# Residual sums formed in PSUM instead of by VectorE additions, and attention biases added by a product with ones

## The reference

```
x = x + 0.5 * moe(layernorm(x))
x = x + attention(layernorm(x))
x = x + 0.5 * moe(layernorm(x))

moe:  affinity = softmax(x @ gate_w)            # 8 experts
      gating, index = top_k(affinity^T, 128)    # each expert picks 128 tokens of a batch
      out = (silu(x_sel @ Wg) * (x_sel @ Wu)) @ Wd
      result = zeros.at[index].add(out * gating)
attention (16 heads of 8):
      aperture, expression = sigmoid(x @ Wa + ba), sigmoid(x @ We + be)
      inner, outer, v = x @ Wi, x @ Wo, x @ Wv
      attn = softmax(inner outer^T / sqrt(8)) * aperture * expression, normalized again
      result = rotate(attn @ v) @ Wout
```

## Time and profile before

| | us |
|---|---|
| median of 3 runs | 478.99 (478.91 to 479.18) |
| the profiled execution | 479.99 |
| its span | 478.3 |
| TensorE busy | 402.9 (84%) |
| VectorE busy | 387.3 (81%) |
| ScalarE busy | 232.1 (49%) |
| GpSimd busy | 54.1 (11%) |

### The profile page before, as it was taken

The page is one execution under the profiler, slowest core; times in us unless marked ns, Lnnn a source line. Parts: engine busy times, 40 slices in busy tenths (PEclk is TensorE's granted clock), DMA queues, the critical chain, the costliest instruction groups (busy, mean ns, idle before and its releaser), DMA issues.

```text
span 478.3 us, 7748 instructions
## 1 busy us (share of the span) xinstructions
PE 402.9 (84%) x2220; PEld 217.0 (45%) x2220; DVE 387.3 (81%) x877; ACT 232.1 (49%) x439; POOL 54.1 (11%) x103
## 2 busy tenths in 40 slices
PE   2705999999788989999999999999979039999995
PEld 1602556776453543333333333334429014567764
DVE  6698977889789888998899899887545889768883
ACT  2400543341432157777777777778762104443322
POOL 4520002212000010000000000000014400011210
PEclk9999999999897669999999999999995559999999
DMA  6100011223077801111111111100200000112103
GB/s 179 46 0 0 1 34 34 66 66 89 16 276 236 325 29 46 47 46 56 49 54 55 52 45 45 45 1 4 66 1 0 0 1 1 34 33 66 45 23 88
DMA packets 25768, 27.49 MB, mean 57 GB/s; under 512 B 3920, under 2 KB 17488, under 8 KB 25680
## 3 DMA queue, kind: packets, MB, share of 16 engines
q1 hardware_dynamic: 25744, 27.20, 18.6%
HBM read 17.08 MB, written 9.98 MB: 57 GB/s over the span
## 4 chain that ended last, share of the span: by engine, by line
PE 76%; DVE 15%; ACT 4%; issue 2%; DMA 1%; DVEq 0%; ACTq 0%
PE ps L1192 14%; PE ps L1202 13%; PE ps L1177 6%; PE ps L1036 6%; PE ps L1074 6%; PE ps L1057 3%; PE ps L1059 3%; PE ps L1058 3%; DVE heads_out L726 3%; DVE neg_max L839 3%; DVE values L723 3%; PE ps L1089 3%; PE ps L1090 3%; PE ps L992 3%; ACT probs L616 2%
## 5 line engine op out<-in xcount | busy, mean ns | idle before, releaser
L839 DVE TENSOR_REDUCE neg_max<-ps 128x1 f32<-128x512 f32 x256 | 160.9, 679 | 14.5 <-PE ps L1177 14.4
L616 ACT ACTIVATE probs<-ps 128x512 f32<-128x512 f32 x256 | 136.8, 601 | 44.1 <-PE ps L1192 42.9
L1177 PE MATMUL ps<-stacks 63*128 63x512 f32 x256 | 106.1, 494 | 3.3 <-DVE neg_max L839 2.4
L1192 PE MATMUL ps<-stacks 64*128 64x512 f32 x256 | 95.1, 463 | 4.7 <-ACT probs L616 4.6
L1192 PEld LDWEIGHTS ps<-stacks 64*128 64x128 f32 x256 | 41.2, 189 | 76.3 <-ACT probs L616 65.6
L1202 PE MATMUL ps<-probs,v_ext 128*32 128x512 f32 x512 | 69.0, 612 | 0.0
L1177 PEld LDWEIGHTS ps<-stacks 63*128 63x128 f32 x256 | 43.6, 195 | 20.0 <-DVE neg_max L839 15.7
L532 ACT CAST stacks<-ps 128x512 fp32r<-128x512 f32 x32 | 17.2, 589 | 67.2 <-PE ps L1036 67.2
L769 DVE TENSOR_TENSOR probs<-slot_row,slot 128x512 f16<-128x512 f16 x64 | 39.2, 681 | 0.1
L458 POOL TENSOR_TENSOR w_lo<-w_gu,w_hi 128x512 fp32r<-128x512 f32 x16 | 20.3, 1275 | 146.2 <-ACT w_hi L517 146.2
L794 DVE TENSOR_TENSOR vae_and_gates<-heads_out,ps 128x512 f32<-128x512 f32 x32 | 21.7, 685 | 16.1 <-ACT heads_out L540 8.3
(11 more groups left out here) (152 smaller groups left out, 556.3 us busy)
## 6 DMA issues: line engine op xcount, KB each, us to landing
stacks<-parts_dram SPq DMA_DIRECT2D x64, 128.0 KB, 2.4
parts_dram<-part_hi SPq DMA_DIRECT2D x8, 512.0 KB, 3.5
parts_dram<-part_lo SPq DMA_DIRECT2D x8, 512.0 KB, 5.2
w_gu<-in_L_ffn_Wg_dram SPq DMA_DIRECT2D x16, 128.0 KB, 2.1
w_gu<-in_L_ffn_Wu_dram SPq DMA_DIRECT2D x16, 128.0 KB, 2.1
wd_sb<-in_L_ffn_Wd_dram SPq DMA_DIRECT2D x16, 128.0 KB, 2.2
x<-in_L_attn_x_dram SPq DMA_DIRECT2D x4, 256.0 KB, 3.7
stacks<-k_rows_dram SPq DMA_DIRECT2D x2, 512.0 KB, 6.7
```

The costliest lines, as they stand in the source:

```text
L616: nc.scalar.activation(probs[:, u // HG, u % HG, :], ps[:, RING + ring_bank(step, u), :], ACT.Exp, scale=SCORE_SCALE).then_inc(probs_ready, 1)
L839: nc.vector.tensor_reduce(neg_max[:, g, col, qt:qt + 1], ps[:, ring_bank(step, u), :], AX.X, ALU.max, negate=True).then_inc(max_taken, 1)
L1177: nc.tensor.matmul(ps[:, ring_bank(step, u), :], q_stack[rows, g, pp, chunk(qt)], k_stack[rows, g, pp, :], start=True, stop=True).then_inc ...
L1192: nc.tensor.matmul(ps[:, RING + ring_bank(step, u), :], k_stack[rows, g, pp, chunk(c)], q_stack[rows, g, pp, :], start=True, stop=True).th ...
```

## The change

Scatter bank b begins as the transposes of x of batch b (16 transposes in place of four products of zeros), and the factor 0.5 moves to copy_down. So the bank holds x plus half of the expert sums, and the transposes back give the new x in banks 4 to 7 (SUM_BANK + b). There is no add_moe. After the first expert stage VectorE takes statistics and normalizes from these banks, and ScalarE copies them to x (copy_x). TensorE projects in other banks, since the sums lie in 4 to 7, and in another order; VectorE's and ScalarE's lists are reordered. The biases are added by a product of a row of ones with the bias row, 32 columns, behind each of the vae products, and ScalarE copies the result (copy_vae). At the end of attention, batch 3's output bank starts with the product of the identity with x, its statistics and its norm are read from there, and VectorE's copy to x, which gives the fourth x_attended, stands behind norm_apply(2, 3). After the last stage VectorE copies three batches and ScalarE the fourth. TensorE's wait for x_attended ahead of logits(1, 0) stays as it was.

```diff
 copy_down:
-    nc.scalar.copy(down_out[:], ps[:, 6, :]).then_inc(down_copied[l], 1)
+    nc.scalar.mul(down_out[:], ps[:, 6, :], 0.5).then_inc(down_copied[l], 1)
 TensorE, experts, ahead of the loop:
+    if l == 1:
+        pe.wait_ge(x_attended, B)
     for b in range(B):
-        nc.tensor.matmul(ps[:, b, :], zeros[:, 0:P], zeros[:], start=True, stop=True)
+        for c in range(C):
+            nc.tensor.matmul(ps[:, b, chunk(c)], x[:, C * b + c, :], ident[:], is_transpose=True,
+                             start=c == 0, stop=True, skip_group_check=True)
 ScalarE, preparation of attention:
+    def copy_x(l, b):
+        act.wait_ge(moe_turned[l], b + 1)
+        if l == 0:
+            act.wait_ge(xn_ready[1], C * (b + 1))
+        nc.scalar.copy(x[:, b * C:(b + 1) * C, :]..., ps[:, SUM_BANK + b, :]).then_inc(x_copied[l], 1)
     root(1, 0)
+    copy_x(0, 0)
     copy_xnT(1, 0)
     root(1, 1)
+    root(1, 2)
     copy_qk_hi(0)
-    root(1, 2)
+    copy_x(0, 1)
     copy_xnT(1, 1)
+    root(1, 3)
+    copy_x(0, 2)
+    copy_qk_hi(1)
     copy_xnT(1, 2)
-    root(1, 3)
-    copy_qk_hi(1)
+    copy_x(0, 3)
     copy_xnT(1, 3)
+    copy_vae(0)
     copy_qk_hi(2)
+    copy_vae(1)
+    copy_vae(2)
     copy_qk_hi(3)
     copy_max_rows(0, 0)
+    copy_vae(3)
 VectorE, preparation of attention:
+    stats_of_sum(0)
+    norm_apply(1, 0, steps, SUM_BANK)
+    stats_of_sum(1)
+    stats_of_sum(2)
+    norm_apply(1, 1, steps, SUM_BANK + 1)
+    split_qk_lo(0)
+    stats_of_sum(3)
+    norm_apply(1, 2, steps, SUM_BANK + 2)
+    norm_apply(1, 3, steps, SUM_BANK + 3)
     split_qk_lo(1)
-    add_bias(1)
     split_qk_lo(2)
-    add_bias(2)
     take_maxima(0, range(MAX_UNITS))
     split_qk_lo(3)
-    take_maxima(1, range(MAX_UNITS // 2))
-    add_bias(3)
-    take_maxima(1, range(MAX_UNITS // 2, MAX_UNITS))
+    take_maxima(1, range(MAX_UNITS))
 TensorE, preparation of attention:
+    QK_BANKS = ((0, 4), (1, 5), (4, 5), (4, 5))
+    VAE_BANKS = ((2, 6), (3, 7), (3, 6), (6, 7))
     project_vae(b):
-        pe.wait_ge(xnT_ready[1], b + 1)
+        pe.wait_ge(xnT_ready[1], (3, 4, 4, 4)[b])
+        if b < 2:
+            sum_bank_free(2 + b)        # xn_ready of the batch, and x_copied
+        if b > 1:
+            pe.wait_ge(vae_ready, 2 * b)
+            last = nc.tensor.matmul(ps[:, VAE_BANKS[b][w], first + D:first + D + 2 * H], ones_row[:],
+                                    bias_row[0:1, D:], start=False, stop=True, skip_group_check=True)
     turn_xn(1, 0)
     project_qk(0)
     turn_xn(1, 1)
+    project_qk(1)
     turn_xn(1, 2)
+    turn_xn(1, 3)
     project_vae(0)
-    project_qk(1)
+    project_qk(2)
     project_vae(1)
-    turn_xn(1, 3)
-    project_qk(2)
     project_vae(2)
 End of attention:
+    in project_out(3), ahead of its wait for combinedT:
+        nc.tensor.matmul(ps[:, OUT_BANK[b], :], ident[:], x[:, b * C:(b + 1) * C, :]..., start=True, stop=True)
+    in add_attention(3), instead of the add:
+        norm_stats(2, b, norm_steps, OUT_BANK[b])
     norm_apply(2, 2, norm_steps)
-    norm_apply(2, 3, norm_steps)
+    norm_apply(2, 3, norm_steps, OUT_BANK[3])
+    nc.vector.tensor_copy(x[:, 3 * C:, :]..., ps[:, OUT_BANK[3], :]).then_inc(x_attended, 1)
```

More of the change, by code:

```diff
@@ L386, in _ @@
             for b in range(B):
-                sp.wait_ge(x_added[1], b + 1)
+                if b < B - 1:
+                    sp.wait_ge(out_rows_ready, b + 1)
+                else:
+                    sp.wait_ge(x_copied[1], 1)
                 sp.dma_start(out[b].rearrange("(c p) d -> p c d", p=P), x[:, b * C:(b + 1) * C, :]).then_inc(out_stored, 16)
@@ L566, in experts @@
                     act.wait_ge(scattered[l], b + 1)
-                    nc.scalar.mul(moeT[:, b, :], ps[:, b, :], 0.5).then_inc(moeT_ready[l], 1)
+                    nc.scalar.copy(moeT[:, b, :], ps[:, b, :]).then_inc(moeT_ready[l], 1)
             act.wait_ge(eps_made, 1)
@@ L638, in _, with norm_stats @@
             experts(1)
+            copy_x(1, B - 1)
         @block.vector
         def _(dve):
-            def norm_stats(n, b, steps):
+            def norm_stats(n, b, steps, bank=None):
                 tiles = range(b * C, (b + 1) * C)
                 for t in tiles:
-                    steps.did(nc.vector.bn_stats(out=stats[:, t, :], in_=x[:, t, :]))
+                    rows = x[:, t, :] if bank is None else ps[:, bank, D * (t % C):D * (t % C) + D]
+                    steps.did(nc.vector.bn_stats(out=stats[:, t, :], in_=rows))
                 steps.settle()
@@ L649, in norm_stats, with norm_apply @@
                     nc.vector.bn_aggr(out=mean_var[:, t, :], in_=stats[:, t, :]).then_inc(var_ready[n], 1)
-            def norm_apply(n, b, steps):
+            def norm_apply(n, b, steps, bank=None):
                 t0 = slice(b * C, (b + 1) * C)
@@ L656, in norm_apply @@
                 for t in range(b * C, (b + 1) * C):
-                    nc.vector.tensor_scalar(xn[:, t, :], x[:, t, :], mean_var[:, t, 0:1], rstd[:, t:t + 1],
+                    rows = x[:, t, :] if bank is None else ps[:, bank, D * (t % C):D * (t % C) + D]
+                    nc.vector.tensor_scalar(xn[:, t, :], rows, mean_var[:, t, 0:1], rstd[:, t:t + 1],
                                             ALU.subtract, ALU.mult).then_inc(xn_ready[n], 1)
@@ L969, in _ @@
             norm_apply(2, 2, norm_steps)
-            norm_apply(2, 3, norm_steps)
+            norm_apply(2, 3, norm_steps, OUT_BANK[3])
+            nc.vector.tensor_copy(x[:, 3 * C:, :].rearrange("p c d -> p (c d)"), ps[:, OUT_BANK[3], :]).then_inc(x_attended, 1)
             route(1)
             experts(1)
-            for b in range(B):
-                add_moe(1, b)
+            for b in range(B - 1):
+                copy_out_rows(b)
         @block.tensor
@@ L1155, in project_vae @@
                     for c in range(2):
-                        f = slice(c * (D + 2 * H), (c + 1) * (D + 2 * H))
-                        last = nc.tensor.matmul(ps[:, 6 + w, f], xnT[:, b, chunk(2 * w + c)], wvae_sb[:], start=True, stop=True)
+                        first = c * (D + 2 * H)
+                        nc.tensor.matmul(ps[:, VAE_BANKS[b][w], first:first + D + 2 * H], xnT[:, b, chunk(2 * w + c)], wvae_sb[:],
+                                         start=True, stop=True, skip_group_check=True)
+                        last = nc.tensor.matmul(ps[:, VAE_BANKS[b][w], first + D:first + D + 2 * H], ones_row[:], bias_row[0:1, D:],
+                                                start=False, stop=True, skip_group_check=True)
                     last.then_inc(vae_projected, 1)
@@ L1276, in project_out @@
             def project_out(b):
+                if b == B - 1:
+                    nc.tensor.matmul(ps[:, OUT_BANK[b], :], ident[:], x[:, b * C:(b + 1) * C, :].rearrange("p c d -> p (c d)"),
+                                     start=True, stop=True, skip_group_check=True)
                 pe.wait_ge(combinedT_ready, b + 1)
@@ L1280, in project_out @@
                 for c in range(C):
-                    last = nc.tensor.matmul(ps[:, OUT_BANK[b], chunk(c)], combinedT[:, b, chunk(c)], w_rot[:], start=True, stop=True)
+                    last = nc.tensor.matmul(ps[:, OUT_BANK[b], chunk(c)], combinedT[:, b, chunk(c)], w_rot[:], start=b < B - 1, stop=True,
+                                            skip_group_check=b == B - 1)
                 last.then_inc(attention_out, 1)
```

68 lines of the change are left out of this document (32 added, 36 removed).

## The result

| | before | changed |
|---|---|---|
| median, us | 478.96 (478.91 to 479.18) | 500.75 (499.31 to 503.69) |
| profiled execution, its span | 479.99, 478.3 | 500.7, 499.0 |
| TensorE, VectorE busy | 402.9, 387.3 | 421.3, 380.2 |

The changed kernel takes 1.0468 times as long, interval [1.0439, 1.0497]. Forecast were 491.3 and a range that ends at 495.5: the direction was right, the size was not. Six points of the two timelines say where the 20.7 us of span arise. Scatter banks are in the first and the last piece; the second and the third, 15.3 us together, are the preparation of attention, the fifth its end.

The account below looks back on a forecast made before the run. TensorE was taken to bound the kernel, through its chain of waits. Terms 1.8 + 3.75 + 1.5 + 0.8 + 4.6 - 0.1 = 12.35 us on the median of 478.99 gave 491.3, range 484.5 to 495.5.

Parts of the forecast that it names:

- what bounds it: Whole kernel: TensorE ends most steps of the chain of waits; in the preparation of attention VectorE waits.
- scatter banks: Both expert stages: sixteen transposes in place of four products of zeros, nothing hides them, +0.90 us a stage, +1.8 for two.
- the logits waiting for the copy: Ahead of logits(1, 0): TensorE waits for VectorE's copy of x, which gives the fourth x_attended, at 366.3 us.
- the loops' period: Expert loops: the period stays unchanged at 6.8 us (423.61 to 430.38).
- almost nothing at the end of the kernel: After the last stage: three VectorE copies and one ScalarE copy replace four adds, -0.1 us (0 to -0.5).
- Rival 3: Preparation of attention: VectorE is the bound, its lighter load decides and hides TensorE's lateness, 477.9 us; chance 0.05.
- xnT(2): Preparation of attention: ready at 137.7 us, where it was there near 134.3 before.
- The order: Preparation of attention: reordered queues put norm_apply(2) behind the split of qk(0) and make xnT(2) late; 1.05 us beside the products.
- the price of the products with ones: project_vae: eight added instructions at 0.11 us each, half hidden, 0.9 a vae (0.3 to 1.7).
- the clock: Preparation of attention: TensorE perhaps at half clock when vae(0) and qk(2) come, +0.8 us (0 to +3).
- The bound itself: Upper price for a product with ones: 0.21 us an instruction at full clock, from logits with float32 stationaries and 8 columns.
- End of attention: From batch 3's output bank to the logits: the copy of x comes late and the whole delay goes through, +4.6 us (3.7 to 5.8).

## Why the prediction missed

- **Right:** what bounds it (TensorE, not VectorE, in the preparation); scatter banks; the logits waiting for the copy; the loops' period (444.34 to 451.11); almost nothing at the end of the kernel. Rival 3, the only one that could have ended faster, fell: VectorE is idle for 8.34 us ahead of its first reduction, and for 2.13 even without the products.
- **Right by luck:** xnT(2) at 138.0 (137.7 forecast). At full clock it comes near 136.3, some 1.4 before the forecast, and half clock from 128 to 138 made up for it. The order, to which the forecast left 1.05 beside the products, came to -0.2.
- **The failed step: the price of the products with ones.** 0.11 an instruction, 0.9 a vae, with bounds of 0.3 and 1.7. Measured 2.05 a vae at full clock and 3.14 at half, beyond the high bound; the first maxima product came 29.2 us behind VectorE's first statistics, not 23. From the earlier trace rows I took a logits product, 0.21 an instruction at either clock, as the upper bound and halved it, since work should hide beside the 160 columns ahead. Nothing hides; the vae product beside it gets up to 0.20 longer, a cost that the sum had no term for. Over four vae this is 9.3 us (6.15 + 3.14) in place of 4.2 (2.7 + 1.5).
- **Mis-sized as well: the clock, +0.8 with 3 at most.** Against an execution at full clock it came to 6.3: 1.8 in qk(0) and qk(1) up to 138, 2.0 in vae(2) (5.24 us instead of 3.2), 2.5 in the maxima and qk(3) behind it (158.61 - 153.01 = 5.60 against 3.10 before). I had priced it at vae(0) and qk(2), where it was full in both traces of the change; without the wait it was at half just there (137 to 147). Sum of the piece ahead of the maxima: 6.15 + 1.8 + 2.0 - 0.2 for the order = 9.75, with 9.65 measured. The 1.8 can't be put down to the change: the kernel before had that half clock in some executions as well. That the rest goes with the products is borne out by the granted clocks of the timed executions (table of the variants); what in them brings the clock down is not shown.
- **The sum of the miss.** Products 5.1 more, clock 5.5 more, order 1.25 less, end of attention 0.84 less: 8.5, where the span missed by 8.35 (20.7 - 12.35). The products at 9.3 and all else as forecast give 496.4 for the median, just beyond 495.5; the clock did the rest.
- **The bound itself was misread.** 0.21 for a logits product "at full clock" rests on rows 5 and 6, where the window says 1.00. At the end of attention, in all traces, products of that kind take 0.12 an instruction at a granted 1.00 and 0.21 at 0.50. At 16.47 us the products ran at the half-clock pace though the window says 1.00; why is open.
- **End of attention, 4.6 against 3.99 (3.76 behind the last logits).** The identity product delayed attention_out by 0.1 beyond the old add's start instead of 0.8; the four tiles from PSUM took 1.36 instead of 1.2.

*The Trainium skill, "SBUF — State Buffer", section "Who interferes with whom", says that a VectorE instruction with at most one SBUF input, outside the two-port modes, does not contend with GpSimd. The trace agrees for the PSUM source: 1.36 us beside GpSimd's cast and subtraction and 1.36 without them (379.89, 125.93), where four tiles from SBUF took 2.38 and 1.11.*

*The Trainium skill, "TensorE: Matmul & The Clock Gate", section "LDWEIGHTS (loading the stationary operand)", which the forecast cited against its low bound, says that loading takes time by the columns of the stationary and not by its rows. The trace agrees in that: at full clock a load of one row takes 182 ns in the mean and a load of 128 rows 188 (138 to 148 us). Its formula, 107 ns for 128 columns, is shorter than both, and the measurement decides. Four products of one row and 160 columns take 1.25 us, as long as four full ones.*

## What to carry to other kernels

Before work is moved from an engine that looks busy to another, ask which of the two the other waits for: here the biases left an engine whose waits could take in all but 0.6 us of them, and went to the engine that it waited for. A small product between large ones is not priced by its columns; measure it in its place. And when one copy becomes the gate of a wait, price what is queued behind it at both clocks: behind the wait of 4.3 to 4.5 us the first sixteen logits instructions took 3.6 us in every trace, without it 1.9. Count the whole kernel too, for a stretch that gained 3.4 in a trace gained the median 0.8.

## What the runs showed of the hardware

- A float32 product over one row, set between products over 128 rows, costs 0.51 us at full clock: 0.20 as a longer slot of the product ahead, about 0.1 for each change of rows, and 0.33 by itself. In a row of their own four such products of 160 columns take 1.25 us, as much as four full ones.
- Two instructions with 8 columns and float32 stationaries take 0.24 us at full clock, 0.43 at half; in the first stage 0.43 though the window says 1.00.
- Normalizing from PSUM costs 0.34 us a tile, with or without GpSimd at work, from SBUF 0.28 alone. Beside GpSimd two of the four tiles from SBUF took 0.63 and 1.31 us, the other two 0.33.
- Half clock behind idle hand-offs at 128 us lasted to 138 in the changed kernel, twice, and was absent in the kernel without its products with ones, which is the same up to there; kernels equal to the one before up to there had it to 132 or to 138. It moves a profile by up to 2 us and is wider than several of the effects asked for: medians over several runs decide, one trace does not.
